# A two-layer network on one core: the mixer's two passes become one run over 32 tiles, and part of the conditioning stage moves into it

## The reference

```python
def _bi_wkv(r, k, v, w, u, time_emb):      # the conditioning: r = x, k = v = a second input f
    tf = sigmoid(sum(time_emb, -1))
    decay = exp(-exp(w)) * (0.5 + 0.5 * tf)
    ek = exp(minimum(k, 30)); ekv = ek * v
    # forward and backward: a = a * decay + ekv, b = b * decay + ek  -> nf, df, nb, db
    euk = exp(minimum(u + k, 30))
    num = nf + nb - ekv + euk * v
    den = df + db - ek + euk
    return sigmoid(r) * (num / maximum(den, 1e-8)) * (0.8 + 0.2 * tf)

def _mamba2_mixer(h, W_in, conv_w, conv_b, dt_bias, A_log, D_param, norm_w, W_out):
    gate, hBC, dt = split(h @ W_in.T)            # 2048, 2048 + 128 + 128, 32 columns
    hBC = silu(causal_conv4(hBC) + conv_b)       # depthwise, 4 taps
    xs, Bm, Cm = split(hBC)                      # 32 heads x 64, 128, 128
    dt = softplus(dt + dt_bias); A = -exp(A_log)
    # per head: state = exp(dt A) * state + (dt x) B^T ;  y = state C
    y = y + D_param * xs
    g = y * silu(gate)
    g = g * rsqrt(mean(g * g) + 1e-5) * norm_w
    return g @ W_out.T

x = x + _mamba2_mixer(_bi_wkv(x, f, f, ...), ...)
x = x + experts(_bi_wkv(x, f, f, ...))           # a second conditioning, other w and u
```

## Time and profile before

| | |
|---|---|
| median of 3 runs | 1437.3 us (1430.36, 1437.3, 1439.8) |
| the profiled execution | 1430.53 us; its span, first to last instruction, 1428.7 us |
| busy over the whole span | TensorE 1208.1 us, VectorE 863.4, ScalarE 585.7, GpSimd 512.9 |
| stage 1 ends, stage 2 begins | at 62.2 and 62.5 us of the span |
| stage 2 ends | at 459.4 us |
| mean granted TensorE clock | 0.952 |

### The profile page before, as it was taken

One profiled execution on the slowest core, in us unless ns is written; L12 is line 12 of the kernel. 1 busy time (PEld: TensorE's weight loads), 2 busy tenths in 40 slices (PEclk: granted clock), 3 DMA queues, 4 the chain that ended last, 5 costly groups with the idle time before them and its releaser, 6 DMA issues. The chain is left out here.

```text
span 1428.7 us, 14494 instructions
## 1 busy us (share of the span) xinstructions
PE 1208.1 (85%) x4614; PEld 642.9 (45%) x4614; DVE 863.4 (60%) x1306; ACT 585.7 (41%) x1732; POOL 512.9 (36%) x499
## 2 busy tenths in 40 slices
PE   0277998688996899999987998978799887987998
PEld 0033454243443444444444655633585346834443
DVE  8789986699993563265236839639750596414222
ACT  1154554354544222222225545647572585700110
POOL 5634576045754110020002827627551375500000
PEclk9999999999998799999997999989899998997999
DMA  6000000000021300000020000030000000000000
GB/s 256 22 1 1 1 1 1 1 0 1 1 83 70 129 1 0 1 0 0 34 111 37 1 0 1 2 140 0 1 2 0 0 1 1 2 0 8 0 0 30
DMA packets 4730, 33.53 MB, mean 23 GB/s; under 512 B 528, under 2 KB 912, under 8 KB 2768
## 3 DMA queue, kind: packets, MB, share of 16 engines
q1 hardware_dynamic: 4656, 32.61, 5.8%
HBM read 31.56 MB, written 1.05 MB: 23 GB/s over the span
## 5 line engine op out<-in xcount | busy, mean ns | idle before, releaser
L780 POOL TENSOR_TENSOR decays<-decays,scores 128x768 f32<-128x768 f32 x64 | 123.3, 1929 | 173.9 <-ACT decays L716 173.6
L1371 POOL TENSOR_TENSOR prob_latent<-prob_latent,inverse_latent 128x128 f32<-128x128 f32 (+1 forms) x128 | 78.6, 637 | 187.1 <-DVE inverse_latent L1361 186.9
L1962 POOL TENSOR_TENSOR euk<-m,weights 128x256 f32<-128x256 f32 x80 | 91.1, 1157 | 91.3 <-DVE m L1983 79.7
L542 PE MATMUL pg<-h,weights 128*128 128x512 f32 (+1 forms) x136 | 66.3, 610 | 65.2 <-PEq L328 62.7
L1067 PE MATMUL ph<-h,weights 128*128 128x512 f32 x256 | 116.8, 601 | 0.0
L542 PE MATMUL px<-h,weights 128*128 128x512 f32 x136 | 73.2, 664 | 32.9 <-DVE conv L852 32.8
L716 ACT ACTIVATE decays<-pcum,neg_cum 128x256 f32<-128x256 f32 (+1 forms) x256 | 87.9, 450 | 12.4 <-PE pcum L595 12.4
L1211 DVE TENSOR_TENSOR mid<-up,ph 128x512 f32<-128x512 f32 x44 | 30.2, 686 | 96.8 <-ACT up L1124 96.8
L1124 ACT ACTIVATE up<-ph 128x512 f32<-128x512 f32 x44 | 26.3, 597 | 140.1 <-PE ph L1067 140.1
L1371 POOL TENSOR_TENSOR prob_gqa<-prob_gqa,inverse_gqa 128x128 f32<-128x128 f32 (+1 forms) x128 | 62.2, 508 | 57.8 <-DVE inverse_gqa L1361 56.1
L852 DVE SCALAR_TENSOR_TENSOR conv<-px,pp,conv 128x510 f32<-128x510 f32 (+2 forms) x102 | 75.2, 737 | 11.8 <-ACT conv L681 9.3
(11 more groups left out here) (317 smaller groups left out, 2955.7 us busy)
## 6 DMA issues: line engine op xcount, KB each, us to landing
weights<-in_w_mixer SPq DMA_DIRECT2D x2, 2048.0 KB, 18.2
weights<-in_w_moe SPq DMA_DIRECT2D x2, 1536.0 KB, 7.7
moe_rest<-in_w_moe SPq DMA_DIRECT2D x2, 1536.0 KB, 13.5
weights<-in_w_gqa SPq DMA_DIRECT2D x1, 3072.0 KB, 9.6
weights<-in_w_gqa SPq DMA_DIRECT2D x1, 2048.0 KB, 14.1
weights<-in_w_moe SPq DMA_DIRECT2D x1, 1920.0 KB, 8.6
weights<-in_w_mixer SPq DMA_DIRECT2D x1, 1536.0 KB, 12.5
weights<-in_w_moe SPq DMA_DIRECT2D x1, 1152.0 KB, 11.9
```

The source lines that it names most:

```text
L542: op = nc.tensor.matmul(out[0:m, :], w[:, col + k * m:col + (k + 1) * m], net.h[:, ds(i * PAIR + k * TOK, TOK)], start=(k == 0), stop=(k = ...
L780: nc.gpsimd.tensor_tensor(decays[:, head % 4], decays[:, head % 4], scores[:], ALU.mult).then_inc(decay_scaled, 1)
L1371: op = nc.gpsimd.tensor_tensor(self.prob[:, slot, cols], self.prob[:, slot, cols], self.inverse[:, slot, t:t + 1].to_broadcast([P, P * (t ...
L1962: op = nc.gpsimd.tensor_tensor(out[:, :, s, :], src[:, :, 1 - s, :], sin[:, None, s, :].to_broadcast([P, 4, HALF]), ALU.mult)
```

## The change

- Stage 1 keeps pair 0's unit and `make_h(0)` alone. Its loads, and the `e` and `ev` of both pairs, stay.
- The mixer is one loop over T = 0 to 36 with 32 tiles, tile T of pair T // 16. Pair 0's drain and pair 1's tiles are the same steps. The order in which each PSUM bank is used is written out in lists (`x_order`, `g_order`, `t_order`, `c_order`) and all waits are counted from them.
- Pair 1's prologue goes into pair 0's tiles: `dt` projection and `softplus` at T = 11, `cum_parts` and B at 12, the transposes, `row_cols` and C at 13, the scores at 15. B and C of pair 1 go through `px`, and their taps and silu stand behind VectorE's other work of the tile.
- Three units run inside the tiles: pair 1's of the first conditioning (then `make_h(1)`), and the two of the second. VectorE takes 3 steps in a tile where T is even or under 6, else 2, from T = 0. GpSimd's four instructions of a unit stand in tiles start + 2, 3, 6, 7, with starts 0, 11 and 22.
- The sum of squares, `root` and `add_to_x` of pair 0 stand at T = 20. ScalarE no longer preloads tables there or for the softplus.
- Buffers that were shared get their own place (`z`, `cum`, `dt`, `root`, `scaled`; `parts`, `scores`, `neg_cum`, `dt_tok` for each pair), so `tanh_gate` no longer waits for `cum_parts`.
- The norm's weight is folded by ScalarE, six instructions in each of the first tiles. `sel` shrinks to 96 x 32, read with a stride of zero. `mix` takes the two heads in turn for each matmul.

```diff
...
-                for step in unit.pool_numerator(pair, pair):
-                    step()
+                if pair == 0:
+                    for step in unit.pool_numerator(0, 0):
+                        step()
...
-            for pair in range(PAIRS):
-                dve.wait_ge(e0_exp, pair + 1)
...
-                make_h(pair)
+            dve.wait_ge(e0_exp, 1)
+            take(steps, 2 * KT)
+            dve.wait_ge(ev_ready, 1)
+            take(steps, len(steps))
+            make_h(0)
...
+DT_STEP, B_STEP, C_STEP, CUM_STEP, TURN_STEP, QUERY_STEP = 11, 12, 13, 12, 13, 15
...
+        units = {1: (CondUnit(net, 0, net.cond_sems), 1),
+                 2: (CondUnit(net, 1, net.cond_sems), 0),
+                 3: (CondUnit(net, 1, net.cond_sems), 1)}
+        UNIT_START = {1: 0, 2: 11, 3: 22}
...
+                pe.wait_ge(decay_scaled, (T + 1) * TILE_HEADS)
+                for b in range(BB):
+                    for r in range(ST):
+                        cols = slice(0, SEQ) if r == 0 else slice(SEQ, TRI)
+                        for hh in range(TILE_HEADS):
...
+                for i in range(PAIRS):
+                    if T == (i + 1) * N + LAG_OUT:
+                        sum_squares(i)
+                if 0 <= T - 1 < TILES:
+                    turn_x(T - 1)
+                if T == N + LAG_OUT:
+                    mix(T - LAG_Y)
+                if 0 <= T - LAG_OUT < TILES:
+                    project_out(T - LAG_OUT)
+                if 0 <= T - LAG_Y < TILES and T != N + LAG_OUT:
+                    mix(T - LAG_Y)
...
+                if T == DT_STEP:
+                    softplus(1)
+                if 0 <= T - LAG_HEADS < TILES:
+                    exp_decay(2 * (T - LAG_HEADS))
+                if T < TILES:
+                    tanh_conv(T)
+                    tanh_gate(T)
+                if 0 <= T - LAG_HEADS < TILES:
+                    exp_decay(2 * (T - LAG_HEADS) + 1)
...
+            for T in range(STEPS + 1):
+                if T < TILES:
+                    taps(T)
+                if T == 0:
+                    cum_parts(0)
+                if T == 1:
+                    row_cols(0)
+                    take_scores(0)
+                if T == DT_STEP:
+                    softplus_in(1)
+                if T == CUM_STEP:
+                    cum_parts(1)
+                if T == TURN_STEP:
+                    row_cols(1)
+                if T == QUERY_STEP:
+                    take_scores(1)
+                if 0 <= T - LAG_Y < TILES:
+                    gated(T - LAG_Y)
+                if T < TILES:
+                    silu_x(T)
+                if 0 <= T - 1 < TILES:
+                    take_x(T - 1)
+                if T < TILES:
+                    silu_gate(T)
+                for step, n in ((B_STEP, "b"), (C_STEP, "c")):
+                    if T == step:
+                        taps((1, n))
+                        silu_x((1, n))
+                for i in range(PAIRS):
+                    if T == (i + 1) * N + LAG_OUT:
+                        add_to_x(i)
+                take(cond, 3 if T % 2 == 0 or T < 6 else 2)
...
```

More of the change, by code:

```diff
@@ L391, in _ @@
                 ALU.mult).then_inc(cols_ready, 1)
-            steps = [unit.vector(link, pair, pair) for pair in range(PAIRS)]
+            steps = unit.vector(link, 0, 0)
             for pair in range(PAIRS):
@@ L398, in _ @@
                 if pair == 0:
-                    take(steps[0], KT)
-            for pair in range(PAIRS):
-                dve.wait_ge(e0_exp, pair + 1)
-                scans = (KT if pair == 0 else 2 * KT) + KT
-                take(steps[pair], scans)
-                dve.wait_ge(ev_ready, pair + 1)
-                take(steps[pair], len(steps[pair]))
-                make_h(pair)
+                    take(steps, KT)
+            dve.wait_ge(e0_exp, 1)
[3 more added lines that the diff above has]
+            make_h(0)
 def condition_input(net, tag):
@@ L914, in add_to_x @@
                 for k in range(KT):
-                    out = net.x[:, ds(i * PAIR + k * TOK, TOK)]
-                    link(v.tensor_tensor(g[:, k, :], pout[k][:], root[:], ALU.mult))
-                    op = v.tensor_tensor(out, out, g[:, k, :], ALU.add)
-                op.then_inc(out_free, 1)
-            for i in range(PAIRS):
-                link = Links(dve, links, i, MIXER_LINKS)
-                cond = unit.vector(link, i, i + PAIRS)
-                taps(i, 0, link)
-                softplus_cum(i, link)
-                taps(i, 1, link)
-                silu_x(i, 0)
-                silu_x(i, 1)
-                for s in range(STEPS):
-                    if s < N:
-                        taps(i, s + 2, link)
-                    if s == 0:
-                        cum_parts(i, link)
-                    if s == 1:
-                        row_cols(i)
-                    if 0 <= s - LAG_Y < N:
-                        gated(i, s - LAG_Y, link)
-                    if s < N:
-                        silu_x(i, s + 2)
-                    if 0 <= s - 1 < N:
-                        take_x(i, s - 1)
-                    if s < N:
-                        silu_gate(i, s)
-                    if s >= 2:
-                        take(cond, 2)
-                assert not cond
-                add_to_x(i, link)
-                link.check()
@@ new lines, in add_to_x @@
+                    out = net.x[:, i * PAIR + k * TOK:i * PAIR + (k + 1) * TOK]
+                    v.tensor_tensor(scaled[:], pout[k][:], root[:], ALU.mult) \
+                        .then_inc(out_free, 1)
+                    dve.wait_ge(out_free, KT * i + k + 1)
+                    link(v.tensor_tensor(out, out, scaled[:], ALU.add))
+            cond = []
+            for turn, (unit, pair) in units.items():
+                cond += unit.vector(link, pair, turn)
+                if turn == 1:
+                    cond.append(partial(make_h, 1))
@@ L952 @@
+            assert not cond
 class Experts:
```

526 lines of the change are left out of this document (304 added, 222 removed).

## The result

The changed kernel takes 1458.7 us (median of 4 runs, 1453.23 to 1459.29), the kernel before 1438.55 in the same comparison: a ratio of 1.0144 (95% interval 1.0113 to 1.0176). It is slower by 20 us. The forecast was 1429, and 1453 was the upper end of its range.

A forecast was written before the change was run, and what follows sets the result against it. VectorE was taken to bound all tiles but those with reciprocals (TensorE's). Savings of 84.8 against 80.9 added gave net -4, taken as -8: 1430.5 to 1422.5 profiled, 1429 after the 6.8 up to the median; range 1398 to 1453.

The forecast's parts named there:

- the second walk's discount: Whole sum: a tile-by-tile walk gave -9 against net -4, as some waits and port time coincide; -8 was taken.
- T = 11: Pair 1's softplus tile: ScalarE's softplus, table loads and decays make VectorE wait 4.5 us before `silu_x` (0 to 7).
- 12 of the 13.6 us back: VectorE's waits for `py` in both pairs: cheaper mix and a third step in every other tile recover 12 us.
- T = 20 and 21: Pair 0's square sum, root and `add_to_x`: `gated(17)` waits 7.3, later steps are held too; together 15.5 us (8 to 22).
- T = 24 and 29: Units 1 and 3 wait for GpSimd's part: `own` 1.5 and `factor` 5, together 6.5 us (0 to 10).
- The port: VectorE's waiting for GpSimd in the tiles: 84 us against 70, so +14 (-10 to +35).
- the first rival: The port doesn't fill further: its total is 60 us, not 84, giving 1405; chance 0.26.
- Stage 1: Stage 1 loses pair 1's unit, the mixer starting after `make_h(0)` instead of `make_h(1)`: 26.7 us less.
- the mix at 1.6: TensorE's mix in each tile, two heads side by side: 1.6 us, 0.6 less than before.
- the unit's bare work at 21.9 + 1.2: Third unit and `make_h(1)` added to VectorE's chain in the tiles: 23.1 us.
- The joint isn't hidden, since each engine's queue is in order: Rival: TensorE idles where VectorE waits, its clock falls, and handovers cost 1.7 times as much: +14, 1443; chance 0.14.
- The 44.1 us "removed": Joint, from taps of tile 15 to those of pair 1's tile 0: 44.1 us go, an ordinary step replacing them.

The follow-up runs named there:

- e9: Changed kernel, with TensorE doing mix(T-3) before x_like(T) in tiles 11 to 15 and 20: 1447.55 us, 1.0085 of the kernel before.
- e7: Changed kernel, with GpSimd's sum of the numerators in stage 1 waiting until VectorE's four sums are done: 1452.88 us, 1.0104 of the kernel before.
- e12: Changed kernel with mix first in six tiles, scores early, softplus late, B and C taps early, GpSimd's stage 1 sum after VectorE's four: 1435.12 us, 1.0003.
- e8: Kernel before, with mix taking its two heads in turn for each matmul: 1432.66 us, 0.9978 of the kernel before.
- e4: Changed kernel, with mix(17) ahead of the square sum and turn_x(19) on TensorE at T = 20: 1448.46 us, 1.0104 of the kernel before.
- e13: Kernel before, pairs apart, with pair 1's unit moved into pair 0's tiles and GpSimd's stage 1 sum after VectorE's four: 1425.99 us, 0.9928.
- e11: Kernel before, with GpSimd's sum in stage 1 after VectorE's four sums, for both pairs: 1429.46 us, 0.9949 of the kernel before.
- e14: Changed kernel with mix, scores, softplus, taps and stage 1 sum reordered, and pair 1's first unit back in stage 1 (joint alone, mended): 1446.48 us, 1.0066.
- e15: Kernel before, with GpSimd's stage 1 sum after VectorE's four in both pairs, and mix taking its two heads in turn: 1427.61 us, 0.9933.

## Why the prediction was wrong

The recorded forecast for the profiled execution was 1422.5 us; it took 1458.66, 36.2 more. The recorded terms give a mixer of 411.0 us (388.2 - 44.1 - 12 - 2 + 80.9), which took 438.4: 27.4 of the 36.2. The start has 6.7, the second walk's discount 4.1, and the rest of the kernel was 2.0 shorter.

- **The step that failed: the waits at the joint.** "T = 11" was priced at 4.5 as a chain on ScalarE, and tiles 12, 13 and 15 at nothing beyond their work; the text ended by naming T = 12 and 13 as the place where an unseen chain could be. The waits were 10.75, 0.8, 6.3 and 9.25 us: +22.7. The chain is TensorE's queue, let go late by VectorE and back at 1.2 GHz, with the mix last in it. e9 shows it by taking these waits away with nothing but that order, and the 4.44 us that then came to light in tile 11 agree with the 4.5 that was computed, for a second chain. What the waits were worth is another number: e9's order alone made the mixer only 4.3 us shorter, since other waits and port time took their place, and all the mends together (e7 to e12) 16.3.
- **"12 of the 13.6 us back".** Outside tiles 11, 12, 13, 15, 20 and 21 and the drain VectorE still waited 13.1 us for `py`, not 1.6: +11.5. With 31 tiles and three or two steps in each, tiles of 6.98 us are followed by tiles with a wait of 2.4: VectorE got ahead of TensorE's floor and gave it back. e8 says the same of the mix: 0.7 us saved a tile took 4.5 us off VectorE's waits.
- **T = 20 and 21** was 15.5; waits of 8.7 before `gated(17)`, 4.0 before the taps of tile 21 and 3.3 before `gated(18)` and the four instructions of `add_to_x` make 18.8: the mechanism was right (e4), 3.3 too small. T = 24 and 29, 6.5, took 2.25 + 4.45 = 6.7.
- **The port**, +14, took +5.6, 8.4 less. For the unit alone the term was right: e13 has +14.8 against e11. The direction of the first rival was right too, and its reason fits: where VectorE waits, GpSimd works unopposed. In e9 the waits are 16.4 us lower and port time is 12 higher; in e12, with the waits mended, it is +15 against the kernel before, of which the packed mix has some part (+6 in e8, which the prediction had at nothing). So term and waits trade: what was gained by mending waits was in part paid at the port, and by these numbers that is why e9 fell short.
- **Stage 1**, -26.7, was -20.0. "The mixer starts after `make_h(0)`" was right; that pair 0's unit would last as before was not, as its sums can come after GpSimd's. e7 and e11 show it in both kernels. That the trace of before was a winning execution could have been asked: its median lay 7 us above it.
- The terms of the mixer so far, +22.7, +11.5, +3.3, +0.2 and -8.4, make +29.3 where it was 27.4 over; the -1.9 between them is not traced.
- **Right:** the mix at 1.6 (1.52), the unit's bare work at 21.9 + 1.2 (work rose by 21.2, with B's and C's the same in both), the rest of the kernel untouched.
- **The rivals.** "The joint isn't hidden, since each engine's queue is in order" is the one that came, with the slow projections that it named, but priced at 1.7 times the two handovers that were known, +14, it gave 1443; the waits of tiles 12, 13 and 15 were not in it. It should have been worked out tile by tile: every step of the handover is a place where TensorE may wait for VectorE and VectorE for the mix behind it.
- **The 44.1 us "removed"** was the premise that failed most widely: e14 gets nothing for them, even mended: it is 19 us above e15, which has them.

What stays open: e14's waits before the taps of tiles 11, 12, 20 and 21 might be mended further by other orders; that wasn't tried, nor was a unit plan that fits the joined tiles. Nor do the runs separate, within a handover's wait, the order of TensorE's queue from its lower clock. e9's gain is measured against the changed kernel of another comparison, in whose profile the sums of stage 1 had lost; the figures by the mixers alone are 438.4 to 434.1 for it, and 438.1 to 421.8 for e7 to e12.

## What to carry to other kernels

A gap between two runs of tiles is worth at most the idle time of the limiting engine, here 24 of 44 us. Set against it the waits that the handover will have inside the tiles, which took all of it here, and what the other engines quietly get done in the gap and would do beside the limiting engine. When one change has several parts, compare runs that differ in one of them: against e11 the joint's loss looks like port time, against e15 it is mostly waiting. When a step of another phase is put into a pipelined tile, ask in each queue what stands between it and the product that the limiting engine needs next, and put that product first in just those tiles. Moving independent work into the tiles and the drain, and leaving the loop as it is, was the part that didn't lose.

## What the runs showed of the hardware

- Two engines whose instructions start 0.15 to 0.16 us apart can order themselves either way in the same code. VectorE's first sum starts first in all 13 places, as at 22.96 us with GpSimd's at 23.11. In four of them GpSimd's 128 x 1024 sum then takes 2.70 us and VectorE's next ones 2.8 each, in the changed kernel 8.9 us for the four instead of 2.5; in the other nine GpSimd's takes 5.18, on no one's path. One wait on GpSimd was worth 0.5% of the kernel (e11) and took away most of its scatter. This is the lock that the Trainium skill ("SBUF — State Buffer", section "Who interferes with whom") describes; which engine gets through had to be measured, and the starts in the traces don't tell it.
- TensorE's clock over the mixer fell from 0.96 to 0.88 in the changed kernel, with the same 1330 matmul records; after idle times of 4.8 to 8.8 us its projections took 3.6 to 3.8 us instead of 1.9. Its mix got cheaper by 0.7 us in each of 32 tiles, and its busy time was 325.7 against 324.7: the lower clock took the gain back. The packed mix in the kernel before (e8, clock 0.94) had brought it to 310.8.
- Two heads in turn bring the 16 passes of a mix to 1.52 us from 2.22, 1.5 times faster. The "Up to 2×" of the Trainium skill ("TensorEngine Tiling (Array Packing)", "Theoretical Speedup"), put on the 2.22 as the prediction did, would make it 1.1 (an estimate); the trace has 1.52. But the passes of the two heads overlapped in part before: against the 2.8 us that the prediction estimates for them one after the other, 1.52 is 1.8 times faster, which is near that limit.
